# ScalarE's program of an attention stage, as a loop over pairs of steps and written out for all steps

## The chip, the cores and the metric

The kernel runs on one core of a Trainium2 chip. A core has five engines with a program each: TensorE (PE; its weight loads are shown apart as PEld), VectorE (DVE), ScalarE (ACT), GpSimd (POOL) and SyncE (SP). They meet only at semaphores. A small q behind an engine's name (ACTq) means its sequencer, which reads the program, sets registers, takes branches and issues DMAs. The metric is the device time of one execution in microseconds (us), the median of several; lower is better.

## The reference, cut to what matters

```
Q, K, V = Wq x, Wk x, Wv x                      # x: 8 batches, 512 channels, 1024 places; 16 heads of 32
att = softmax((Q K^T / sqrt(32) + b) masked by cond_2048)
y   = (att V) transposed                        # 8 x 512 x 1024
q   = per-row int8 quantisation of y            # absmax of a row / 127
out = x + f16(q W8^T * in_scale * w_scale + bias)
```

All matrix products of attention are computed in 32-bit floats; the quantised product runs in bf16.

## The kernel before, in words

The kernel has two stages, one after the other. `project` (to about 560 us) computes Q, K and V and stores them in DRAM. `attend` (line 504 on, from about 560 us to the end) does the rest in 32 steps: a step is one batch and one group of four heads. Line numbers here are those of the kernel before; behind line 867 those of the changed kernel are higher by one.

A step has 64 slots t. A slot is one pair of key tile (128 keys) and head, for one half of the queries (512). In slot t TensorE computes a block of scores (`scores`, L689) into one of three PSUM banks; ScalarE takes its exponential into `probs` in SBUF (`exps`, L798), which frees the bank; every fourth slot TensorE multiplies the four finished blocks of a key tile with V (`weigh`, L716, 8 matmuls into `pv`). Between them, in each slot, TensorE computes half of a pair of score blocks in the other orientation (`row_max`, L127), of which VectorE takes the row maxima (`reduce_max`, L136). These belong partly to this step and partly to the next.

In slots 23 and 55 the maxima are turned (L734), ScalarE and VectorE split them into two parts (`high_max` L803, `low_max` L877), and SyncE stores both parts with two small DMAs (L609) as rows of `q_stack`. TensorE waits for these rows in slots 32 and 0 (`max_rows`): the scores of that half need them. GpSimd sums the probabilities of a half (`add`, L987), after two accumulating DMAs of 1 MB that it issues itself (`begin_pair`, L971). In slot 51 TensorE does the quantised product for the step before (`ffn`, L749).

ScalarE also issues most loads (`loads`): K for the next step in slots 0 to 2 (L109), two bias rows (L115), V in slot 8 (L832), the second half of Q in slots 24 to 26 (L102), the residual in slot 30 (L843) and the first half of Q for the step after next in slots 38 to 40 (L102). It does these in its own order, between exponentials: while its sequencer issues a DMA, the next exponential isn't started.

Every engine runs its own order of work, written out by hand in a function `step(s, par, ...)`. `all_steps` (L585 to L594) calls it: steps -1, 0, 1 and 2 are written out, steps 3 to 28 are a loop of 13 rounds over two steps each (an odd one and an even one), and steps 29 to 32 are written out again. In the loop the step number is a register, so wait values and DMA addresses are computed by register instructions. TensorE, VectorE, ScalarE and GpSimd all use `all_steps`; SyncE has a loop of its own (L635).

Of the kernel before, what the change touches and what calls it, by code (L numbers as in the profile page):

```python
# [30 lines left out]
STEPS = B * G  # L31
# [472 lines left out]
def attend(nc, x, qk_d, v_d, bias_d, fw, ws_rep, fb_rep, out,  # L504
# [3 lines left out]
    with ExitStack() as ctx:  # L508
# [70 lines left out]
        def ring_of(par, use):  # L579

            return ring[(len(USES) * par + PLACE[use]) % 2]
# [3 lines left out]
        def all_steps(eng, body):  # L585

            body(-1, 1, main=False, prev=False)
            body(0, 0, prev=False)
            body(1, 1)
            body(2, 0)  # L590
            with eng.Fori(1, STEPS // 2 - 2) as pair:
                body(2 * pair + 1, 1)
                body(2 * pair + 2, 0)
            body(STEPS - 3, 1)  # L594
            body(STEPS - 2, 0)
            body(STEPS - 1, 1, ahead=False)
            body(STEPS, 0, main=False, ahead=False)
# [186 lines left out]
        def _(act):  # L784
# [15 lines left out]
            def high_max(s, chunk, buf):  # L800
                act.wait_ge(maxT_done, 2 * s + chunk + 1)
                wait(act, max_rows[chunk], MAX_ROWS * s)
                nc.scalar.activation(max_hi[:, chunk, :], buf[0:CHUNK, N:N + P], ACT.Copy).then_inc(max_hi_done, 1)  # L803

            def take_y(s, half):
                act.wait_ge(pv_done, QH * TT * s + (half + 1) * TT)
                wait(act, y_done, 2 * (s - 1) + half + 1)
                nc.scalar.activation(y_raw[:, half, :], pv[:, :], ACT.Copy).then_inc(y_raw_done, 1)

            def round_rows(s, half):  # L810

                cols = slice(half * N, (half + 1) * N)
                act.wait_ge(inv_done, s + 1)
                nc.scalar.activation(y[:, cols], y[:, cols], ACT.Identity, bias=magic[:, 0:1], scale=inv_scale[:, 0:1]).then_inc(rounded, 1)
# [26 lines left out]
            def load_res(s):  # L841
                wait(act, out_stored, 32 * s)
                act.dma_start(res[:, :], x[bass.ds(s * P, P), :]).then_inc(res_loaded, 16)  # L843

            def step(s, par, prev=True, main=True, ahead=True):
                for t in range(UNITS):
                    if main:
                        exps(s, t)
                        loads(s, par, t, prev, ahead)
                    elif t == 0 and prev:  # L850
                        load_res(s - 1)
                    if t == 3 and prev:
                        take_y(s - 1, 1)
                    if t == SUMS_1 and main:
                        high_max(s, 1, ring_of(par, ("extra", SUMS_1)))
                    if t == 35 and main:
                        take_y(s, 0)
                    if t in (37, 39) and prev:
                        round_rows(s - 1, (t - 37) // 2)
                    if t in (41, 43) and prev:  # L860
                        make_ints(s - 1, (t - 41) // 2)
                    if t == SUMS_0 and ahead:
                        high_max(s + 1, 0, ring_of(par, ("extra", SUMS_0)))

            act.wait_ge(const_set, 5)
            act.wait_ge(stack_set, 4)
            all_steps(act, step)

        @block.vector
        def _(dve):  # L870
# [225 lines left out]
```

## Time and profile before

| | |
|---|---|
| time, median of 3 runs (lowest to highest) | 2454.46 us (2453.87 to 2454.95) |
| the profiled execution, own time | 2455.09 us |
| its span (first to last instruction) | 2453.3 us |
| granted TensorE clock, mean | 0.99 |
| PE matmul busy | 2391.8 us, 97% |
| DVE busy | 1562.5 us, 64% |
| ACT busy | 1355.8 us, 55% |
| POOL busy | 1673.3 us, 68% |
| exponentials (L798) | 2048, 607 ns each |

Busy time of PE says that matmuls were in flight, not that PE was at its peak. What matters for a change in one engine's program is where TensorE waits for it, so the rows further down are taken from the chain of waits (the work that ended last, followed back from the end), from the timeline and from the list of one source line's instructions.

### The profile page before, as it was taken

How to read it: one execution, taken by the hardware profiler on the slowest of the kernel's cores; microseconds unless marked ns; L12 is line 12 of the kernel's file. 1: busy time of each engine (PE TensorE's matmuls, PEld its weight loads, DVE VectorE, ACT ScalarE, POOL GpSimd, SP SyncE). 2: the span in 40 equal slices, each digit the busy share in tenths (PEclk: the TensorE clock that was granted, in tenths of full speed). 3: DMA queues.
4: the chain of work that ended last, by engine and by line, in shares of the span. 5: the costliest groups of instructions: out<-in, count | busy, mean ns of one | idle time of the engine just before them, and what ended most of it. 6: DMA issues, size and time to landing. Idle time of an engine off the chain costs nothing.

```text
span 2453.3 us, 40026 instructions
## 1 busy us (share of the span) xinstructions
PE 2391.8 (97%) x12344; PEld 1342.7 (55%) x12376; DVE 1562.5 (64%) x1683; ACT 1355.8 (55%) x2536; POOL 1673.3 (68%) x677
## 2 busy tenths in 40 slices
PE   8999999997999999999999999999999999999997
PEld 7888888884444444444444444444444444444442
DVE  3311111155777777777777777777777777777771
ACT  3222222214666666666666666666666666666664
POOL 3322223414788888887788888887888888887786
PEclk9999999998999999999999999999999999999997
DMA  6655555465776667766777766667776667767751
GB/s 241 252 201 194 214 197 197 152 201 129 154 160 154 153 149 157 161 155 151 160 157 159 155 154 156 150 149 157 160 155 156 147 152 161 155 153 157 156 112 37
DMA packets 143540, 396.90 MB, mean 162 GB/s; under 512 B 14584, under 2 KB 50424, under 8 KB 127296
## 3 DMA queue, kind: packets, MB, share of 16 engines
q0 software_dynamic: 18144, 132.13, 26.9%
q10 hardware_dynamic: 49312, 130.80, 22.5%
q1 hardware_dynamic: 75968, 132.74, 14.8%
q8 instruction: 34, 0.56, 0.1%
q14 instruction: 82, 0.67, 0.1%
HBM read 161.51 MB, written 100.93 MB: 107 GB/s over the span
## 4 chain that ended last, share of the span: by engine, by line
PE 67%; issue 3%; DMA 3%; DVE 1%; ACT 1%; ACTq 1%; POOL 1%; SPq 0%; POOLq 0%; DVEq 0%
PE score L689 22%; PE pv L716 19%; PE ring L127 17%; PE ring L749 4%; DMA q_stack<-max_lo 3%; PE ring L726 2%; PE ring L729 2%; ACT probs L798 1%; DVE neg_max L136 1%; PE ring L740 1%; ACTq L102 1%; PE ring L734 0%; SPq L609 0%; DVE absmax L898 0%; POOL k_stack L121 0%
## 5 line engine op out<-in xcount | busy, mean ns | idle before, releaser
L798 ACT ACTIVATE probs<-score 128x512 f32<-128x512 f32 x2048 | 1085.7, 607 | 574.4 <-PE score L689 555.5
L136 DVE TENSOR_REDUCE neg_max<-ring 128x1 f32<-128x1024 f32 x1024 | 1210.4, 1221 | 242.2 <-PE ring L127 230.3
L689 PE MATMUL score<-q_stack,k_stack 100*128 100x512 f32 x2048 | 880.1, 432 | 30.3 <-DMA q_stack<-max_lo 15.8
L987 POOL TENSOR_TENSOR acc<-acc,probs 128x2048 f32<-128x2048 f32 x189 | 867.0, 4587 | 27.0 <-DMA probs<-probs 13.1
L127 PE MATMUL ring<-k_stack,q_stack 98*128 98x512 f32 x2048 | 811.0, 396 | 0.3 <-DVE neg_max L136 0.2
L689 PEld LDWEIGHTS score<-q_stack,k_stack 100*128 100x128 f32 x2048 | 388.8, 190 | 522.3 <-ACT probs L798 353.8
L716 PE MATMUL pv<-probs,v_in 128*32 128x512 f32 x4096 | 548.6, 608 | 0.0
L127 PEld LDWEIGHTS ring<-k_stack,q_stack 98*128 98x128 f32 x2048 | 390.7, 191 | 64.5 <-DVE neg_max L136 0.8
L987 POOL TENSOR_TENSOR acc<-probs 128x2048 f32<-128x2048 f32 x63 | 288.8, 4584 | 86.1 <-DMA probs<-probs 86.1
L479 POOL TENSOR_TENSOR q_stack<-x_raw,k_stack 128x1024 fp32r<-128x1024 f32 x28 | 67.7, 2456 | 293.1 <-ACT k_stack L364 293.1
L971 POOL DMA_DIRECT2D probs<-probs x126 | 108.6, 862 | 189.0 <-PE pv L716 182.3
L716 PEld LDWEIGHTS pv<-probs,v_in 128*32 128x32 f32 x4096 | 80.7, 108 | 185.9 <-issue 97.6
L435 DVE TENSOR_TENSOR part_lo<-score,part_hi 128x512 fp32r<-128x512 f32 x24 | 16.4, 691 | 179.5 <-ACT part_hi L389 179.5
L491 POOL TENSOR_TENSOR part_lo<-k_scaled,part_hi 128x512 fp32r<-128x512 f32 x64 | 83.3, 1320 | 55.0 <-ACT part_hi L392 55.0
L749 PE MATMUL ring<-fw,qT 128*128 128x512 bf16 x480 | 111.1, 385 | 6.2 <-issue 4.9
L1012 POOL TENSOR_TENSOR half<-prod,fb_rep 128x512 f16<-128x512 f32 x64 | 81.6, 1275 | 47.9 <-DVE prod L921 47.9
L291 PE MATMUL ring<-k_stack,w_hi 128*128 128x512 f32 x256 | 101.4, 396 | 0.0
L291 PE MATMUL ring<-k_stack,w_lo 128*128 128x512 f32 x256 | 101.2, 395 | 0.0
L291 PE MATMUL ring<-q_stack,w_hi 128*128 128x512 f32 x256 | 101.2, 395 | 0.0
L392 ACT ACTIVATE part_hi<-k_scaled 128x512 fp32r<-128x512 f32 x64 | 39.0, 628 | 111.3 <-DVE k_scaled L446 80.6
L921 DVE SCALAR_TENSOR_TENSOR prod<-ring,scale,ws_rep 128x512 f32<-128x512 f32 x64 | 48.1, 751 | 81.6 <-PE ring L749 81.6
L884 DVE STREAM_TRANSPOSE sums_turned<-ring 128x512 f32<-128x512 f32 x64 | 45.9, 717 | 83.7 <-PE ring L729 83.7
(95 smaller groups left out, 2031.1 us busy)
## 6 DMA issues: line engine op xcount, KB each, us to landing
probs<-probs POOLq DMA_DIRECT2D x126, 1024.0 KB, 7.8
k_stack<-qk_part ACTq DMA_DIRECT2D x93, 512.0 KB
q_stack<-qk_part ACTq DMA_DIRECT2D x183, 256.0 KB, 4.7
qk_part<-part_hi SPq DMA_DIRECT2D x64, 512.0 KB, 2.6
qk_part<-part_lo SPq DMA_DIRECT2D x64, 512.0 KB, 3.5
v_steps<-v_out SPq DMA_DIRECT2D x64, 256.0 KB, 2.2
res<-x ACTq DMA_DIRECT2D x32, 512.0 KB, 5.0
out<-res SPq DMA_DIRECT2D x64, 256.0 KB, 2.1
```

The lines of the kernel that those rows point to most:

```text
L127: mm = pe.matmul(ring[:, half * N:(half + 1) * N], q_stack[par][0:ROW_MAX, chunk, h, qt * P:(qt + 1) * P], k_stack[par][0:ROW_MAX, h, half ...
L136: nc.vector.tensor_reduce(neg_max[:, pair // CHUNK, pair % CHUNK:pair % CHUNK + 1], ring[:, :], AX_X, ALU.max, negate=True).then_inc(neg_m ...
L291: return pe.matmul(bank[:, :], lhsT, rhs, start=(k == 0), stop=(k == 3 * CT - 1))
L479: nc.gpsimd.tensor_tensor(x_lo[par][:, a, :], x_raw[:, a, :], x_hi[par][:, a, :].bitcast(F32), ALU.subtract).then_inc(x_lo_done, 1)
L491: nc.gpsimd.tensor_tensor(part_lo[:, g % 2, th * N:(th + 1) * N], k_scaled[:, i % 2, :], part_hi[:, g % 2, th * N:(th + 1) * N].bitcast(F3 ...
L689: pe.matmul(score[score_bank(t)][:, :], k_stack[par][0:ROWS, h, kt * P:(kt + 1) * P], q_stack[par][0:ROWS, half, h, :], start=True, stop=T ...
L716: mm = pe.matmul(pv[h * DH:(h + 1) * DH, :], v_in[:, par, kt % TT, h * DH:(h + 1) * DH], probs[:, kt % RING, h, :], start=(kt % TT == 0), ...
L749: mm = pe.matmul(buf[:, cols], qT[:, tt, :], fw[:, tt, cols], start=(tt == 0), stop=(tt == TT - 1))
L798: nc.scalar.activation(probs[:, kt, h, :], score[score_bank(t)][:, :], ACT.Exp).then_inc(exp_done, 1)
L971: pool.dma_start(probs[:, b, :, :], probs[:, a, :, :], accum_op=ALU.add).then_inc(pair_done[i], 16)
L987: nc.gpsimd.tensor_tensor(acc[:, half, :, :], first, probs[:, tile, :, :], ALU.add).then_inc(acc_done, 1)
L1012: nc.gpsimd.tensor_tensor(half16[:, half, :], prod[:, half, :], fb_rep[:, cols], ALU.add).then_inc(half_done, 1)
```

## The change

ScalarE doesn't call `all_steps` any more. It calls the same `step` once for each s from -1 to 32, with an ordinary number for s. The flags come out as `all_steps` has them. The other four engines keep their loops. The computation, the order of exponentials, copies and DMA issues and the conditions of all waits stay the same.

```
-            all_steps(act, step)
+            for s in range(-1, STEPS + 1):
+                step(s, s % 2, prev=s > 0, main=0 <= s < STEPS, ahead=s < STEPS - 1)
```

With numbers in place of a register the instructions that computed wait values and addresses are gone, and with the loop its branch. ScalarE's program of the stage gets longer: 1444 rows where the whole kernel's listing had 741.

The first place is ScalarE at the seam of two rounds of the loop, between an even step and the odd step behind it. Before, the last exponentials of the loop body and what closes it (the branch leads back to the row `L591 ISA` of the second listing):

```order
L798 ACTIVATE probs<-score 128x512
L797 REGISTER_ALU
L798 ACTIVATE probs<-score 128x512
L591 REGISTER_ALU
L591 COMPARE_AND_BRANCH
```

and the head of the loop body, where the odd step begins:

```order
L591 ISA
L73 ISA
L797 ISA
L798 ACTIVATE probs<-score 128x512
L109 ISA
L109 DMA k_stack<-qk_part 32x4x1024
L797 REGISTER_ALU
L798 ACTIVATE probs<-score 128x512
L109 DMA k_stack<-qk_part 32x4x1024
```

Now the same seam, from slot 55 of a step (L803) over its end into the next one:

```order
L803 ACTIVATE max_hi<-ring 16x128
L798 ACTIVATE probs<-score 128x512 x9
L109 DMA k_stack<-qk_part 32x4x1024
L798 ACTIVATE probs<-score 128x512
L109 DMA k_stack<-qk_part 32x4x1024
L798 ACTIVATE probs<-score 128x512
L109 DMA k_stack<-qk_part 32x4x1024
L798 ACTIVATE probs<-score 128x512
L808 ACTIVATE y_raw<-pv 128x512
```

The branch and the register rows are gone; the exponentials and the three K loads stand in the same order. (The L803 shown is that of slot 55; the nine exponentials behind it are slots 56 to 63 and slot 0 of the next step.)

The second place is ScalarE in slots 23 to 26, where it splits the maxima and issues three loads of Q. Before, in the loop:

```order
L803 ACTIVATE max_hi<-ring 16x128
L73 REGISTER_ALU x2
L797 REGISTER_ALU
L798 ACTIVATE probs<-score 128x512
L102 ISA
L102 DMA q_stack<-qk_part 32x4x512
L797 REGISTER_ALU
L798 ACTIVATE probs<-score 128x512
L102 DMA q_stack<-qk_part 32x4x512
L797 REGISTER_ALU
```

Now:

```order
L803 ACTIVATE max_hi<-ring 16x128
L798 ACTIVATE probs<-score 128x512
L102 DMA q_stack<-qk_part 32x4x512
L798 ACTIVATE probs<-score 128x512
L102 DMA q_stack<-qk_part 32x4x512
L798 ACTIVATE probs<-score 128x512
L102 DMA q_stack<-qk_part 32x4x512
L798 ACTIVATE probs<-score 128x512 x4
```

Here too only register instructions have gone; each Q load still stands between two exponentials. On TensorE, VectorE, GpSimd and SyncE nothing moved.

## Rows read from the trace of the kernel before

**Rows 1.** The page: part 1 (engine, busy us, share, instructions) and part 4.

```profile
PE 2391.8 (97%) x12344; PEld 1342.7 (55%) x12376; DVE 1562.5 (64%) x1683; ACT 1355.8 (55%) x2536; POOL 1673.3 (68%) x677
...
PE 67%; issue 3%; DMA 3%; DVE 1%; ACT 1%; ACTq 1%; POOL 1%; SPq 0%; POOLq 0%; DVEq 0%
```

**Rows 2.** Chain of waits, 974 to 979 us: start us, us, what.

```profile
974.23 2.41 issue
976.63 0.07 ACTq L591
...
976.91 0.61 ACT probs L798
...
977.56 0.50 PE score L689
```

**Rows 3.** Instructions of L591, 973 to 978 us: engine, operation, ns, first start.

```profile
L591 ACTq COMPARE_BRANCH  x1: 54/54/54, 974.2 to 974.2; - x1
...
L591 DVEq COMPARE_BRANCH  x1: 67/67/67, 974.4 to 974.4; - x1
L591 DVEq FUSED_REGOPS  x1: 85/85/85, 974.7 to 974.7; - x1
L591 ACTq FUSED_REGOPS  x1: 68/68/68, 976.6 to 976.6; - x1
```

**Rows 4.** Timeline of PE: start, us, engine, line, what, [idle before, releaser].

```profile
974.22 1.06 PE L716 MATMUL pv<-probs,v_in 128*32 128x512 f32 x8
...
977.56 0.50 PE L689 MATMUL score<-q_stack,k_stack 100*128 100x512 f32 x1 [0.68 <-ACT probs L798]
...
987.43 1.06 PE L716 MATMUL pv<-probs,v_in 128*32 128x512 f32 x8
...
1032.70 1.07 PE L716 MATMUL pv<-probs,v_in 128*32 128x512 f32 x8
...
1044.91 1.06 PE L716 MATMUL pv<-probs,v_in 128*32 128x512 f32 x8
```

**Rows 5.** Chain of waits, whole span: the quantised product, slot 51 of each step.

```profile
670.76 3.40 PE ring L749 x15
...
728.45 3.40 PE ring L749 x15
...
786.64 3.40 PE ring L749 x15
...
844.78 3.40 PE ring L749 x15
...
903.21 3.40 PE ring L749 x15
...
960.85 3.40 PE ring L749 x15
...
2237.77 3.40 PE ring L749 x15
...
2296.25 3.40 PE ring L749 x15
...
2354.02 3.40 PE ring L749 x15
```

**Rows 6.** Timeline, slots 26 to 32 of steps 4, 6, 29 and 30.

```profile
824.04 1.55 ACTq L102 DMA_DIRECT2D q_stack<-qk_part  x1
826.34 0.50 PE L689 MATMUL score<-q_stack,k_stack 100*128 100x512 f32 x1 [0.66 <-ACT probs L798]
...
940.59 0.78 ACTq L102 DMA_DIRECT2D q_stack<-qk_part  x1
...
944.58 0.49 PE L689 MATMUL score<-q_stack,k_stack 100*128 100x512 f32 x1 [0.24 <-DMA q_stack<-max_lo]
...
2280.03 0.50 PE L689 MATMUL score<-q_stack,k_stack 100*128 100x512 f32 x1 [1.21 <-DMA q_stack<-max_lo]
...
2333.51 1.45 ACTq L102 DMA_DIRECT2D q_stack<-qk_part  x1
```

## The prediction

> **What bounds the kernel now.** I read the page first. TensorE's matmuls are in flight for 97% of the span and PE is 67% of the chain that ended last; ScalarE is busy for 55% [rows 1]. So ScalarE isn't short of throughput, and a shorter program on it is worth only what TensorE loses by waiting for it. The chain's second entry, 3% of "issue", is time in which an engine waited for nothing that the profile shows. The reader should look for where it stands.
>
> In the chain it stands once in each round of the loop. At 974.23 us there are 2.41 us of issue, then ScalarE's sequencer works on L591 (the loop), the exponential of slot 0 starts at 976.91, and TensorE's score of slot 3, which waits for that exponential's bank, starts behind it at 977.56 [rows 2]. The list of the loop line's instructions shows whose time this is: ScalarE's branch is at 974.2 and its next instruction at 976.6, 2.4 us later, while VectorE takes its own branch at 974.4 and goes on at 974.7 [rows 3]. The hole belongs to ScalarE's branch alone and not to loops as such.
>
> The Trainium skill, "Runtime: NRT & Kernel Launch", section "Instruction fetch mechanics", says that a taken branch to a place outside the engine's small instruction window waits for a transfer of that page, and that kernels therefore prefer to be unrolled. The 2.4 us on the engine with the long body and 0.3 us on VectorE, whose body is shorter, fit it.
>
> **What the hole costs TensorE.** ScalarE's sequencer reaches the branch before its exponentials are through, so part of the 2.4 us is covered. TensorE's timeline gives the rest. A key tile is four slots. Across the seam four tiles take 974.22 to 987.43 = 13.21 us; across the middle of the loop body, between an odd and an even step, where ScalarE does the same work without a branch, four tiles take 1032.70 to 1044.91 = 12.21 us [rows 4]. The idle time before slot 3's matmul is 0.68 us, and the rest is pipelining that is lost. So one branch costs 1.00 us. The loop has 13 rounds, of which 12 end in a taken branch: 12.0 us at most.
>
> **What the change adds or moves.** No exponential, copy or DMA issue moves. The register instructions between exponentials go; most lay under exponentials. I cost them at nothing, and the bounds are in the step times below, since steps 2, 29 and 30 are written out already and hold none of them. What comes instead is a longer program to read, which I also take from those steps. Nothing new waits.
>
> **What is late next.** If ScalarE is in time at slot 0, TensorE runs 1 us ahead of where it was, and GpSimd's and SyncE's transfers don't all move with it. I therefore don't add up savings but take whole steps from the chain, where the quantised product stands once in each step at slot 51, so that a difference of two starts is one step [rows 5]:
>
> - Odd step behind a taken branch (step 5): 903.21 - 844.78 = 58.43 us.
> - Even step behind such a step (step 6): 960.85 - 903.21 = 57.64 us.
> - Steps in the loop with no taken branch in or just before them: step 3, 786.64 - 728.45 = 58.19; step 4, 844.78 - 786.64 = 58.14.
> - Steps written out: step 2, 728.45 - 670.76 = 57.69; step 29, 2296.25 - 2237.77 = 58.48; step 30, 2354.02 - 2296.25 = 57.77.
>
> The branch costs 1.00 us, but step 5 is only 0.29 longer than step 4, which has no branch before it. Something else is late in slots 26 to 32. The timeline shows two things there. In step 4 the third load of Q is 1.55 us in issue on ScalarE (824.04) and TensorE waits 0.66 us for the exponential behind it; in step 6 the same issue takes 0.78 us, and TensorE waits 0.24 us for the rows of maxima instead; in step 30, written out, the issue takes 1.45 us; in step 29 TensorE waits 1.21 us for the rows of maxima [rows 6]. So ScalarE's issue and SyncE's transfer stand side by side as the next limits, both fed by how busy the queues are. Part of what the branch costs is now time in which they catch up, and that part doesn't come back.
>
> **The sum.** The 26 steps 3 to 28 take 2237.77 - 728.45 = 1509.32 us [rows 5]. Changed, all 26 are written-out steps without a branch. The nearest rows are steps 2 and 30, 57.69 and 57.77, mean 57.73: 26 x 57.73 = 1501.0, which is 8.3 us less. Step 29 is the third written-out step and 0.75 us over that mean. I let two of the 26 be like it, plus 1.5 us; it is one of three before, but the only one whose maxima were that late. That leaves 6.8, say 7 us. The stages outside stay. The profiled execution took 2455.09 us; less 7 is 2448.1. The median of the runs is 0.63 below the profiled one, so the changed kernel's median should be 2447.5 us, 0.28% less.
>
> Bounds: all 26 steps like step 6 and a little better (the whole 12.0 us returned) gives 2442.5. All like steps 3 and 4 (mean 58.17) gives 26 x 58.17 = 1512.4, 3.1 us more: 2457.5. All like step 29 gives 26 x 58.48 = 1520.5, 11.2 us more: 2465.6. The value taken is nearest to the written-out steps 2 and 30, because they are the same code as all steps will be and stand in the same surroundings.
>
> **Rivals.**
>
> 1. All of it returns: 12 x 1.00 us, median 2442.5. For it: steps like 6 show that slots 26 to 32 can be nearly free. Against it: step 6 stands behind a step that was delayed, and steps 3, 4 and 30, which don't, have the long third issue.
> 2. The middle of the step takes it all back: every step is like 3 and 4, median 2457.5, or between those and the forecast. For it: these two are the only pair in a row without any branch stall in the steady part, and what they show may be how queues settle when nothing relieves them. Against it: they still have register instructions around the issues, and steps 2 and 30 are 0.4 us shorter. Half-way between (57.95 a step) it is 2453, no change to speak of.
> 3. Slower, by one mechanism: the rows of maxima land late in most steps, as in step 29, because ScalarE's now continuous reading of new program adds transfers beside GpSimd's accumulating DMAs. Price 0.75 us a step over the forecast, up to 2465.6; it decides against the change once the mean step is over 58.24 us (1509.32 + 4.9 over 26), which is two steps in three like step 29. Against it: steps 2 and 30 read new program too and don't show it.
> 4. The stall at the seam isn't the branch's but that of a new step's first work, and stays: 2454.5. Against it: the seam in the middle of the body has the same work and no hole [rows 4].
>
> On rival 3, the Trainium skill, "DMA: Bandwidth & Descriptors", section "Queues, rings and completion order", says that each DMA engine goes round the queues that have work, a packet at a time. By that rule every page of program read in slots 16 to 32 would make one engine's share of the accumulating DMA late, and a transfer is as late as its latest share. No row here shows such a read beside a late landing. How often it would fall there decides between the forecast and this rival.
>
> **Chances.** Forecast (5 to 10 us less) 0.52; rival 1 (over 10 less) 0.15; rival 2 (4.9 less to 4.9 more) 0.22; rival 3 (over 4.9 more) 0.07; rival 4 0.04. This kernel's measurement can tell about 0.2%, 4.9 us, from no change. So faster: 0.52 + 0.15 = 0.67, less 0.03 for the forecast's own edge near 5 us: 0.64. Same: 0.22 + 0.04 + 0.03 = 0.29. Slower: 0.07. The range goes from 2442.0, just under the full return, to 2455.0, which takes in most of rival 2.
>
> **What would show each step.** The branch: in the chain the 2.4 us issue once in 116 us is gone, and four key tiles across any step's start take 12.2 us; ScalarE's list has no L591 compare-and-branch in this stage. If a hole of over 1 us shows elsewhere on ScalarE, program reading isn't hidden. The middle of the step: distances between the quantised products should be near 57.7, odd and even alike, in place of 58.43 and 57.64 in turn. If they are near 58.15, rival 2 holds, and the third Q issue will be about 1.5 us with TensorE behind it; near 58.5 with waits of over 1 us for the rows of maxima, rival 3. The forecast is wrong in its reasoning, even with a right time, if TensorE doesn't gain at the seam, or if slots 26 to 32 don't wait longer than they do now in even steps.

## The result, and the profile after

| | before | after |
|---|---|---|
| time, median of 5 runs (lowest to highest) | 2453.87 us (2452.07 to 2454.95) | 2440.84 us (2438.5 to 2442.08) |
| the profiled execution, own time | 2455.09 us | 2440.84 us |
| its span | 2453.3 us | 2439.0 us |
| granted TensorE clock, mean | 0.99 | 0.993 |

The changed kernel takes 0.9947 of the time before [0.9936, 0.9958]: 13.0 us or 0.53% less. I had forecast 2447.5 us with a range from 2442.0 to 2455.0. The direction was right, the size wrong by a factor of two, and the time lies outside the range, 1.2 us below its lower end. Ratios and medians in this document leave out one run, of `q_late_loop`, which took 2618.68 us at a mean granted clock of 0.847.

The page of the changed kernel, with the lines that answer to [rows 1] and the queue on which ScalarE's program is read (queue, kind: packets, MB, share):

```profile
PE 2387.2 (98%) x12376; PEld 1341.0 (55%) x12376; DVE 1560.4 (64%) x1683; ACT 1346.3 (55%) x2536; POOL 1672.1 (69%) x677
...
q14 instruction: 40, 0.33, 0.0%
...
PE 67%; DMA 4%; issue 2%; POOL 2%; DVE 2%; ACT 0%; SPq 0%; ACTq 0%; POOLq 0%; DVEq 0%
```

and the same queue on the page of the kernel before:

```profile
q14 instruction: 82, 0.67, 0.1%
```

"Issue" has fallen from 3% to 2% of the chain, ACT and ACTq from 1% each to nothing. The written-out program isn't more reading: 40 packets here, where the loop took 82, since the loop read its body anew in each round.

The chain of waits of the changed kernel, whole span, at the quantised product of each step (start, us, what). The first, third, fourth and last rows answer to those of [rows 5]:

```profile
729.50 3.56 PE ring L749 x16
787.12 3.56 PE ring L749 x16
845.11 3.56 PE ring L749 x16
902.43 3.56 PE ring L749 x16
960.01 3.56 PE ring L749 x16
1017.84 3.56 PE ring L749 x16
...
2225.41 3.56 PE ring L749 x16
2284.19 3.56 PE ring L749 x16
2341.89 3.56 PE ring L749 x16
```

Steps 3 to 28 take 2225.41 - 729.50 = 1495.91 us, where they took 1509.32 [rows 5]: 13.4 us less, as much as the medians differ. The mean step is 57.54 us. By differences of all starts, odd steps fell from 58.41 to 57.47, even ones from 57.70 to 57.60: what the branch had cost has gone from the steps behind it, and next to nothing has come back.

The timeline of the changed kernel (start, us, engine, line, what, [idle before, releaser]): two of TensorE's products with V around the start of step 7, which is the seam of [rows 4], then the third load of Q and the wait behind it in step 7, and the same load in step 19:

```profile
973.58 1.07 PE L716 MATMUL pv<-probs,v_in 128*32 128x512 f32 x8
...
985.79 1.06 PE L716 MATMUL pv<-probs,v_in 128*32 128x512 f32 x8
...
997.42 1.51 ACTq L102 DMA_DIRECT2D q_stack<-qk_part  x1
...
999.63 0.50 PE L689 MATMUL score<-q_stack,k_stack 100*128 100x512 f32 x1 [0.41 <-ACT probs L798]
...
1688.26 0.78 ACTq L102 DMA_DIRECT2D q_stack<-qk_part  x1
```

Four key tiles across the seam take 985.79 - 973.58 = 12.21 us, exactly what they take in the middle of the old loop body, where they took 13.21 at the seam [rows 4]. The long third issue of [rows 6] is there in step 7 with its 0.41 us of waiting, and not in step 19.

I summed TensorE's records over steps 3 to 28 by the slots in which the time lies. Slots 28 to 35 mean the eight intervals from the start of slot 27's score block to that of slot 35's:

| steps 3 to 28, us | before | after | difference |
|---|---|---|---|
| slots 28 to 35, sum of 26 steps | 168.37 | 169.19 | +0.8 |
| of it per odd step | 6.32 | 6.43 | +0.11 |
| of it per even step | 6.63 | 6.59 | -0.05 |
| slots 39 to 43 | 95.1 | 93.5 | -1.6 |
| everywhere else | | | -12.6 |
| in all | 1509.32 | 1495.91 | -13.4 |

"Everywhere else" is the seam: 12.5 of the 12.6 us are lost in front of slots 3 and 4. Take the time from slot 59's score block to that of slot 7 of the next step, once for each of the 26 steps. Before, it is 10.10 to 10.40 us in front of the 12 odd steps that stand behind a taken branch, and 9.15 to 9.19 in front of the other 14. Among the 14 are all 13 even steps, which run such register instructions at that place too, with no branch among them. After, all 26 take 9.16 to 9.31. So the loss at the seam goes with the branch, and the register instructions show no part in it.

One more difference lies in the two profiles alone. A row by stretches of each kernel (window, us, then busy us of PE, PEld, DVE, ACT and POOL, granted clock, DMA share, GB/s), in step 31. Before, with the seam of step 7 ahead of it for use further down:

```profile
974.20:976.60 2.40, 2.40 (x15) 1.22 (x14) 1.70 (x3) 0.57 (x2) 2.40 (x1) 1.00 0.01 3
...
2395.20:2407.60 12.40, 12.40 (x36) 3.95 (x36) 0.25 (x2) 9.32 (x17) 12.11 (x3) 0.50 0.00 1
```

After, a stretch that includes the same work:

```profile
2379.70:2397.00 17.30, 13.67 (x71) 4.86 (x70) 1.76 (x4) 14.18 (x28) 16.29 (x5) 1.00 0.14 41
```

The execution of before that was profiled had TensorE at half its clock for 13.7 us there, which cost it 3.7 us by the intervals of its key tiles; the one of after hadn't. The first experiment below shows the same drop in a kernel with the gain, so it belongs to an execution and not to the change. Steps 3 to 28 lie before it, and their 13.4 us don't contain it.

### The profile page after: what moved, and what is told of

Its sections match the earlier page's. It is cut to its first block, busy times and chain, and to the rows that moved or that the text cites. A ratio compares the mean times of both kernels' runs of the same rounds, so it can differ in the third digit from the quotient of the medians.

```text
span 2439.0 us, 37390 instructions
## 1 busy us (share of the span) xinstructions
PE 2387.2 (98%) x12376; PEld 1341.0 (55%) x12376; DVE 1560.4 (64%) x1683; ACT 1346.3 (55%) x2536; POOL 1672.1 (69%) x677
## 4 chain that ended last, share of the span: by engine, by line
PE 67%; DMA 4%; issue 2%; POOL 2%; DVE 2%; ACT 0%; SPq 0%; ACTq 0%; POOLq 0%; DVEq 0%
PE score L689 21%; PE pv L716 18%; PE ring L127 18%; PE ring L749 4%; DMA q_stack<-max_lo 4%; PE ring L726 2%; PE ring L729 2%; DVE neg_max L136 1%; PE ring L740 1%; POOL acc L988 1%; PE ring L734 0%; DMA probs<-probs 0%; POOL acc L1000 0%; ACT probs L798 0%; SPq L609 0%
## 5 line engine op out<-in xcount | busy, mean ns | idle before, releaser
L798 ACT ACTIVATE probs<-score 128x512 f32<-128x512 f32 x2048 | 1074.7, 604 | 576.4 <-PE score L689 559.5
L689 PE MATMUL score<-q_stack,k_stack 100*128 100x512 f32 x2048 | 875.8, 429 | 23.9 <-DMA q_stack<-max_lo 16.6
L749 PE MATMUL ring<-fw,qT 128*128 128x512 bf16 x512 | 117.8, 384 | 0.9 <-DVE qT L917 0.9
```

Of the source, the lines that this page charges most:

```text
L689: pe.matmul(score[score_bank(t)][:, :], k_stack[par][0:ROWS, h, kt * P:(kt + 1) * P], q_stack[par][0:ROWS, half, h, :], start=True, stop=T ...
L749: mm = pe.matmul(buf[:, cols], qT[:, tt, :], fw[:, tt, cols], start=(tt == 0), stop=(tt == TT - 1))
L798: nc.scalar.activation(probs[:, kt, h, :], score[score_bank(t)][:, :], ACT.Exp).then_inc(exp_done, 1)
```

## Experiments

Each was run beside the kernel before on the same chip. The medians of before there were 2454.25 us (beside `one_round`, `four_steps`, `seam_52` and `q_late`), 2452.94 us (beside `seam_20`, `q_late_loop`, `pe_out` and `dve_four`), 2454.09 us (beside `sp_loop`, `sp_out` and `dve_six`) and 2454.16 us (beside `q_late_pe`). The label stands in the title of each.

**One round of a loop (`one_round`).** Is it the branch, or the register instructions in the loop, that cost time? This kernel was meant to keep registers for all waits and addresses of steps 3 to 28, without a taken branch.

```
-            all_steps(act, step)
+            with act.Fori(1, 2) as once:
+                for j in range(STEPS - 6):
+                    step((STEPS - 6) * once - (STEPS - 9) + j, (j + 1) % 2)
```

(Steps -1 to 2 and 29 to 32 are written out around it, here and in the next ones.)

> ScalarE's steps 3 to 28 stand in a loop of one round, 26 steps long: the step number is a register and all register instructions of the old loop are there, but no branch is ever taken. Theory A (the taken branch is the loss, 12 times 1.00 us, and register instructions cost next to nothing): within 2 us of the written-out kernel, so 11.5 to 13.5 us below the kernel before, about 2441.5. Rival B (a good part of the gain comes from the register instructions between exponentials and DMA issues, since the gain was 13.0 us and not 7): steps 3 to 28 stay 0.15 to 0.4 us longer each, 4 to 10 us above the written-out kernel, 2445 to 2451. In the trace both expect no 2.4 us of issue; A expects 57.5 to 57.6 us a step, B 57.7 to 58.1.

Measured: 2442.86 us (2440.71 to 2443.39), ratio 0.9948 [0.9934, 0.9961]. Its chain of waits at the quantised products of steps 2 and 28:

```profile
729.73 3.56 PE ring L749 x16
...
2225.81 3.56 PE ring L749 x16
```

1496.08 us, against 1495.91 written out. But the experiment doesn't do what it was built for. These are the sequencer's instructions of the line that computes the wait values of the exponentials (L797, from 728 to 2240 us), first in the kernel before, then in `one_round`, and then all that `one_round` has of its loop's line:

```profile
L797 ACTq ALU_OP  x1627: 35/35/44, 743.9 to 2236.6; - x181
...
L797 ACTq EVENT_SEMAPHORE  x419: 38/38/38, 733.6 to 2237.9; - x140
...
L869 ACTq MOVE  x1: 42/42/42, 743.2 to 743.2; - x1
...
L869 ACTq COMPARE_BRANCH  x1: 48/48/48, 2239.3 to 2239.3; - x1
```

The changed kernel has the same 419 waits there, and none of either has register arithmetic. A loop of one round was turned into the written-out program, with one branch at its end that isn't taken. So `one_round` is a second sample of the change, and a close one (0.2 us in 26 steps), and says nothing about register instructions. What parts the two is the comparison of seams above, and `sp_loop` and `sp_out` further down, where branches and register instructions stay and the hole doesn't: there the two together are worth 1.3 us. Put on the branches alone, the difference to the kernel before is (1509.32 - 1496.08) / 12 = 1.10 us each. The granted clock was 0.51 in this profile too in step 31 (2383 to 2397 us).

**Four steps to a round (`four_steps`).** Five taken branches in place of twelve.

```
+            with act.Fori(1, 7) as four:
+                for j in range(4):
+                    step(4 * four - 1 + j, (j + 1) % 2)
```

> ScalarE's loop has four steps in a round and six rounds, so five taken branches in place of twelve; it is otherwise the old loop, steps 27 to 32 are written out. Theory A (each taken branch costs 1.0 to 1.1 us, whatever stands behind it): 5 x 1.05 = 5.3 us above the written-out kernel, 2446, or 7.5 below the kernel before. Rival C (a delayed step leaves the queues emptier and gives part back in slots 26 to 32 of this and the next step, as the prediction had it): the steps without a branch are then longer, 57.9 or more, and the time is 2448 or more. The branch is expected once in 231 us with a hole of about 2.4 us.

Measured: 2448.32 us, ratio 0.9973 [0.9963, 0.9984]. The hole stands in its chain of waits once in four steps:

```profile
975.75 2.41 issue
```

Steps 3 to 28 take 1502.92 us, 6.8 more than with one round, which is 1.4 us for each of the five branches: 1.05 at the seam, the rest mostly in slots 39 to 47. So the loss at the seam follows the number of branches: this loop keeps the register instructions of 24 steps, and only the five seams with a taken branch cost. The median is 2.3 us above what theory A had and stands in the range of rival C, but not by C's mechanism: from step 5 to step 27, steps without a branch in front took 57.3 to 57.8 us, and C needed 57.9 and more.

**The seam in slot 52 (`seam_52`).** The same loop of two steps, turned, so that the branch stands behind slot 51 of the odd step, where SyncE's and GpSimd's transfers are under way.

```
-            def step(s, par, prev=True, main=True, ahead=True):
-                for t in range(UNITS):
+            def step(s, par, prev=True, main=True, ahead=True, first=0, last=UNITS):
+                for t in range(first, last):
...
+            step(3, 1, last=SEAM)
+            with act.Fori(1, STEPS // 2 - 2) as pair:
+                step(2 * pair + 1, 1, first=SEAM)
+                step(2 * pair + 2, 0)
+                step(2 * pair + 3, 1, last=SEAM)
+            step(STEPS - 3, 1, first=SEAM)
```

> ScalarE's loop of two steps a round with twelve taken branches as before, but turned so that the branch stands behind slot 51 of the odd step, where TensorE does the quantised product and ScalarE waits over 3 us for scores anyway. Theory A (the branch costs because nothing covers its 2.4 us at slot 0): the hole is still in ScalarE's program but no longer on the chain, and the kernel is within 2 us of the written-out one, 2440 to 2443. Rival D (reading the loop's head again adds transfers, 42 more instruction reads than the written-out kernel by the page's queue rows, and these cost by themselves): 3 to 6 us above the written-out one, 2444 to 2447. If it is like the kernel before, 2454, the branch isn't the cause.

Measured: 2453.1 us (2452.22 to 2456.66), ratio 0.9996 [0.9987, 1.0005]: the time of before. I had written that such a time would clear the branch. It doesn't, since the branch's hole didn't stay as it was. The chain of waits has a longer one than [rows 2]:

```profile
1015.89 6.40 issue
```

and its stretch shows why it costs TensorE no more than it does, and what else was going on:

```profile
1015.90:1020.80 4.90, 4.90 (x27) 2.19 (x27) 2.52 (x4) 0.52 (x2) 1.91 (x2) 1.00 1.04 214
```

TensorE had other work for these 4.90 us. The DMA share is 1.04, where it was 0.01 in the hole of before (the first stretch of before, above). In the records of the DMA queues the read of the next piece of program starts 4.92 us after the branch here and 0.93 us in before. Steps 3 to 28 take 1509.68 us. Slots 28 to 35 fall to 164.02 us in all (even steps 6.23 us each, in place of 6.59), and everything else takes 18.8 us more than with one round, 1.6 a branch, nearly all of it in front of slots 55 and 56. So the giving back that I had forecast is real, but for a branch in this place, and it's the even steps that have it: 5.2 of 18.8 us. What is left is 13.6 us, 1.1 a branch, as in the kernel before.

**The seam in slot 20 (`seam_20`).** The same edit with another number, so that the branch stands ahead of the Q loads, with the accumulating DMAs under way and no quantised product for TensorE to be busy with.

```
+            SEAM = 20
```

> ScalarE's loop turned so that its branch stands behind slot 19 of the odd step: no pause of ScalarE there beyond the usual 1 us a key tile, and GpSimd's accumulating DMA in flight (DMA share 0.9 to 1.0 at that place of the step, against 0.01 at the old seam). Theory F (the 2.4 us at slot 0 and the 6.4 us at slot 52 are the same read of program, which waits behind data in the DMA queues): the hole is 4 to 7 us here, TensorE loses it less 1.4 us, 12 times, which is 30 to 65 us more than the written-out kernel: 2471 to 2506. Rival G (the 6.4 us of slot 52 had to do with something at that slot, and the read takes 2.4 us elsewhere): 1.0 us a branch, 2452 to 2455.

Measured: 2521.67 us, ratio 1.0282 [1.0268, 1.0297], 2.8% slower, and above what either theory had. The chain of waits:

```profile
994.67 6.14 issue
```

the stretches under the hole and behind it:

```profile
994.70:999.00 4.30, 2.62 (x15) 1.18 (x14) 3.44 (x5) 0.51 (x2) 0.86 (x1) 1.00 1.01 208
...
1001.00:1004.50 3.50, 2.74 (x10) 0.70 (x10) 1.22 (x1) 2.08 (x4) 3.50 (x1) 0.61 0.91 190
```

and the timeline there:

```profile
1001.76 0.80 PE L689 MATMUL score<-q_stack,k_stack 100*128 100x512 f32 x1 [4.44 <-ACT probs L798]
...
1002.92 1.94 PE L716 MATMUL pv<-probs,v_in 128*32 128x512 f32 x8
```

The hole is 6.2 us, nearly as long as in slot 52, with the DMA share at 1.01 (the read starts 4.66 us after the branch). So its length goes with the traffic in the three places tried; that part of the expectation held. The price didn't. By the chain's products in slot 51 steps 3 to 28 take 1577.17 us (2304.70 - 727.53), 6.8 us a branch. That is more than the hole: TensorE is idle for 4.44 us, and then its clock is granted at half for 3.4 to 6.8 us each time. The score block behind the gap takes 0.80 us and the eight products with V 1.94 us, where they took 0.50 and 1.06 [rows 4].

**Q loads late (`q_late`).** The table of slots says that 6.13 us, the shortest that any step shows for slots 28 to 35, is missed by 0.4 us a step. This is the changed kernel with the three loads of slots 24 to 26 in slots 32 to 34.

```
-                if ahead and t in (24, 25, 26):
-                    load_q(act, qk_d, q_stack, s + 1, 1 - par, 1, t - 24, q2_loaded)
+                if ahead and t in (32, 33, 34):
+                    load_q(act, qk_d, q_stack, s + 1, 1 - par, 1, t - 32, q2_loaded)
```

> The written-out kernel, with ScalarE's three loads of the second half of Q moved from slots 24, 25, 26 to slots 32, 33, 34. It takes away both things that are late in slots 26 to 32: the long third issue, and traffic beside the rows of maxima. If these are the next limit (the prediction's second step), slots 28 to 35 take 6.13 to 6.3 us in place of 6.5 on the mean, and 29 steps give 6 to 11 us: 2430 to 2435. Rival E (the accumulating DMA of GpSimd alone decides when the rows of maxima land, and the third issue is a mere witness): even steps keep 6.5 us there and the kernel gains under 3 us, 2438 to 2441. It can be slower, 2443 or more, if the Q loads now push the first half of Q or the accumulating DMAs of the second half.

Measured: 2424.28 us (2423.79 to 2427.12), ratio 0.9878 [0.9863, 0.9893], 30 us below before and 6 us below the least that was expected. The chain of waits:

```profile
724.51 3.56 PE ring L749 x16
...
2210.62 3.56 PE ring L749 x16
```

Steps 3 to 28 take 1486.1 us, 9.8 less than with the change alone. Slots 28 to 35 are 6.13 to 6.19 us in every step from 3 to 28, and step 29 is 57.20 us, where it was 58.78. Another 7 us came outside these steps: 1.0 before step 0, 4.0 in steps 0 to 2 (step 0 alone 53.8 in place of 57.7), 2.0 from step 29 on. So what was late in slots 26 to 32 hangs on these three loads. Whether it is ScalarE's stop for the issues or the traffic of the loads beside the rows of maxima isn't shown, since the edit takes away both. By place it is about half each: of the 9.7 us that slots 28 to 35 lose, 5.1 are in front of slots 30 and 31, which wait for exponentials, and 4.7 in front of slot 32, which waits for the rows.

**Q loads late, with the loop (`q_late_loop`).** The kernel before with only this edit: is the branch still worth its 1.1 us when nothing can take it back?

> The kernel before, loop and all, with the three Q loads moved from slots 24 to 26 to slots 32 to 34. With slots 26 to 32 waiting for nothing, nothing can be given back there. Theory A (a branch costs TensorE 1.0 to 1.1 us, and the middle of the step neither gave back nor took much): 12 x 1.05 = 12.6 us above the written-out kernel with late Q loads (2424.3), 2436 to 2438. Rival C (the middle of the step gave part of the branch back): the difference is clearly larger than the 13.0 us between the two kernels of this case, 15 us or more, 2439 or more. Slots 28 to 35 are expected at 6.13 to 6.2 us in all steps.

Measured: 2438.61 us (2435.63 to 2439.61), ratio 0.9938 [0.9925, 0.9951]. The chain of waits:

```profile
725.63 3.56 PE ring L749 x16
...
2225.69 3.56 PE ring L749 x16
```

1500.06 us, 14.0 more than without the loop: 1.16 us for each of 12 branches, against 1.10 in the kernel before. The medians differ by 14.3. The time lies between what the two theories expected, close to that of a branch that costs 1.1 us whatever the middle does. Slots 28 to 35 were 168.37 us before and are 159.47 here, so the three loads cost 8.9 us in 26 steps with the loop and 9.7 without it: nearly the same. The two edits add up: 0.53% and 0.62% alone, 1.22% together.

**TensorE's program written out too (`pe_out`).** In both kernels step 29 is long (58.48 us [rows 5] and 58.78) and has a 16 KB read of TensorE's program 20 us behind its start. If such reads hurt, more of them hurt more.

```
-            all_steps(pe, step)
+            for s in range(-1, STEPS + 1):
+                step(s, s % 2, prev=s > 0, main=0 <= s < STEPS, ahead=s < STEPS - 1)
```

> The written-out kernel with TensorE's program written out for all steps too. TensorE's loop had no hole at its branch, so nothing is gained there; its program is then read anew through the whole stage, in reads of 16 KB about every 17 to 20 us. Theory H (a read of program that falls into the 17 to 26 us behind a step's start makes the accumulating DMA and the rows of maxima late, as in step 29, whose slots 28 to 35 took 7.5 us before and 7.8 after): about every second step has such a read, slots 28 to 35 take 7 us or more there, and the kernel is 5 to 20 us slower than the written-out one, 2446 to 2460. Rival I (reads of program cost nothing, and step 29 is long for another reason): 2439 to 2443, and slots 28 to 35 stay at 6.5 us on the mean.

Measured: 2437.43 us (2436.15 to 2439.89), ratio 0.9942 [0.9929, 0.9955]; 3.1 us below the 2440.51 us of `dve_four` on the same chip, which (further down) has the time of the changed kernel. That is below the ranges of both theories. The theory that more reads of TensorE's program cost more time is false: there are 93 packets on that queue in place of 34, two or three in each step, 0.5, 12.6, 26, 36 or 52 us behind its start, and steps 3 to 28 take 1494.5 us. The chain of waits shows where it gained:

```profile
2222.67 3.56 PE ring L749 x16
...
2280.08 3.56 PE ring L749 x16
```

Step 29 is 57.41 us, 1.4 less: its reads now fall at 12.6 and 36 us. Step 31 lost 1.0 us too, in slots 28 to 35, where its read at 21 us is gone.

**VectorE's loop with four steps to a round (`dve_four`).** VectorE's loop has 189 instructions a round and its hole is 0.3 us [rows 3], ScalarE's has 419 and 2.4 to 2.7. Size, or engine? This is the changed kernel with `four_steps`'s loop on VectorE, 373 instructions.

> The written-out kernel, with VectorE's loop at four steps a round in place of two (about 190 instructions a round before, 380 now; ScalarE's old loop had 419 and a hole, VectorE's had none). Theory J (a branch is free as long as the loop's head is still held by the sequencer, and the hole comes with a body that is too long, on any engine): VectorE's instruction behind its branch comes 2.3 to 2.7 us later in place of 0.12 us, five times, and TensorE waits for a row of maxima there, 0.5 to 1.5 us each: 2.5 to 7 us slower than the written-out kernel. Rival K (the hole is peculiar to ScalarE): 0.12 us at VectorE's branch and no difference in time.

Measured: 2440.51 us, ratio 0.9949 [0.9935, 0.9964], the time of the changed kernel. The instructions of the loop's line, on VectorE's sequencer (engine, operation, ns, first start):

```profile
L956 DVEq COMPARE_BRANCH  x1: 74/74/74, 974.6 to 974.6; - x1
L956 DVEq FUSED_REGOPS  x1: 85/85/85, 974.9 to 974.9; - x1
```

0.3 us, as before. So 373 instructions are still at hand when the branch goes back.

**VectorE's loop with six steps to a round (`dve_six`)**, 557 instructions. It ran once, so its time, 2442.0 us, isn't compared.

```
+            with dve.Fori(1, 5) as six:
+                for j in range(6):
+                    step(6 * six - 3 + j, (j + 1) % 2)
```

> The written-out kernel with VectorE's loop at six steps a round: about 560 instructions a round; with four steps it was 374 and there was no hole. Theory J' (the hole comes when a round is longer than what a sequencer holds, and that lies between VectorE's 374 and ScalarE's 419): a hole of 1 to 3 us, or over 5 if data transfers are under way, at each of VectorE's three taken branches (about 1090, 1435 and 1780 us). Rival K (peculiar to ScalarE): 0.12 us there as before.

```profile
L956 DVEq COMPARE_BRANCH  x1: 74/74/74, 1089.1 to 1089.1; - x1
L956 DVEq FUSED_REGOPS  x1: 85/85/85, 1091.9 to 1091.9; - x1
```

2.8 us from branch to next instruction, on another engine (2.8 to 3.1 at its three branches). The hole goes with the body's length and isn't peculiar to ScalarE.

The same trace shows something more. VectorE's longer program is read at places of its own, and in steps 10, 16 and 22 one such 8 KB read starts 20.2 to 20.3 us behind the step's start. The third load of Q in step 8, which has no such read, and in step 10:

```profile
1055.32 0.96 ACTq L102 DMA_DIRECT2D q_stack<-qk_part  x1
...
1170.29 1.57 ACTq L102 DMA_DIRECT2D q_stack<-qk_part  x1
```

In the three steps that issue takes 1.57 to 1.65 us and slots 28 to 35 take 6.89 to 6.96; in the other even steps from 6 to 26 it takes 0.89 to 0.99 and they take 6.34 to 6.44. The same three steps of the changed kernel have no such read, and take 6.59, 6.58 and 6.49.

**All loads issued by SyncE, with the loop (`sp_loop`).** ScalarE's loads (K, bias, V, Q, residual) move to SyncE's program, the second half of Q late; all loops stay, SyncE's with its last steps written out. ScalarE's body has 355 instructions, register instructions included. The main parts of the edit:

```
-                        loads(s, par, t, prev, ahead)
...
+                if main and ahead:
+                    wait(sp, score_done, UNITS * s)
+                    for k in range(3):
+                        load_k(sp, qk_d, k_stack, s + 1, 1 - par, k, k_loaded)
...
+                    sp.wait_ge(score_done, UNITS * s + UNITS // 2 + 1)
+                    for k in range(3):
+                        load_q(sp, qk_d, q_stack, s + 1, 1 - par, 1, k, q2_loaded)
```

> The kernel before, loops and all, with all of ScalarE's loads (K, bias rows, V, Q, residual) issued by SyncE instead, the Q loads of the second half behind slot 32. ScalarE's loop body is then about 355 instructions in place of 419, branch and register instructions kept. Theory J' (length decides): no hole at ScalarE's twelve branches (under 0.3 us), slots 28 to 35 at 6.13 us, 2420 to 2428. Rival K: the hole stays 2.4 us, and the kernel is 11 to 13 us above the next one, 2433 to 2440.

Measured: 2427.43 us (2423.4 to 2427.67), ratio 0.9887 [0.9871, 0.9904]. The instructions of the loop's line:

```profile
L591 ACTq COMPARE_BRANCH  x1: 45/45/45, 969.4 to 969.4; - x1
...
L591 ACTq FUSED_REGOPS  x1: 68/68/68, 969.6 to 969.6; - x1
```

0.24 to 0.26 us in all twelve rounds, and no read of ScalarE's program in the steady rounds. Steps 3 to 28 take 1487.45 us. By itself this kernel would leave open whether the shorter body or the missing DMA issues closed the hole; VectorE's two sizes answer that.

**The same, ScalarE written out (`sp_out`).**

> As the one with SyncE's loads, with ScalarE's program written out. Theory J': equal to the looped one within 2 us, since there is nothing left to gain from writing out, 2420 to 2428. Rival K: 11 to 13 us faster than the looped one. Against the written-out kernel with late Q loads on ScalarE (2424.3) both expect 0 to 4 us less, since ScalarE no longer stops for issues.

Measured: 2425.37 us (2424.15 to 2425.64), ratio 0.9883 [0.9867, 0.99]; steps 3 to 28 take 1486.10 us. The change of this document, made on a kernel whose loop body is short enough, is worth 1.3 us by the traces, 0.1 a branch, and nothing that the intervals tell apart. That 1.3 us is all that twelve held branches and the register instructions of 26 steps cost together in this kernel. Against `q_late` I had expected 0 to 4 us less; it is 1.1 more, which the intervals don't tell apart from nothing.

**Both edits, TensorE written out (`q_late_pe`).**

> The written-out kernel with the Q loads in slots 32 to 34 and TensorE's program written out too. TensorE's writing out alone was worth 3.4 us on the median, of which 1.4 us is step 29 and 1.4 us the slots 28 to 35 of steps 3 to 28. Theory L (it acts only where a read of program meets the accumulating DMA and the rows of maxima, and late Q loads have taken the waiting there away): nothing left, 2423 to 2426 like the kernel with late Q loads alone (2424.3). Rival M (something else is saved): 2 to 4 us less, 2420 to 2422.

Measured: 2424.19 us (2422.6 to 2426.26), ratio 0.9875 [0.9858, 0.9891], the time of late Q loads alone. What `pe_out` gained up to step 30, it gained in slots 26 to 32, and there is nothing left there (steps 3 to 28 take 1486.47 us). Step 31 still gains: its slots 28 to 35 take 5.5 us in place of 6.6. The versions with late Q loads, `q_late`, `q_late_pe` and `sp_out`, are the fastest and aren't told apart.

## Why the prediction was off, step by step

**What bounds the kernel: right.** The page, the chain's "issue" once a round and the branch's instructions named the place. 12.5 of the 13.4 us went from the twelve seams behind a taken branch, and the seams in the middle of a round, with such register instructions and no branch, had nothing to lose. `four_steps` has the loss five times, and `sp_loop` keeps branches and register instructions and loses the hole. Rival 4 (the stall is that of a new step) is out.

**What the hole costs TensorE: right, a little low.** I had 1.00 us and 12.0 in all; at the seam it is 12.5, 1.04 a branch, and 1.10 with what it takes with it elsewhere. Four tiles across the seam take the 12.2 us that I had put down as the sign.

**What the change adds: right.** The register instructions cost nothing at the seams, and with twelve branches at most 1.3 us in all in `sp_loop`. My own bound for them, the written-out steps 2, 29 and 30, was none, as the sum below shows. The longer program added no hole anywhere on ScalarE.

**What is late next: this is the term that was wrong.** I had about 5 us of the 12 come back in slots 26 to 32, and 0.8 us did. The two things I saw there, the long third Q issue and the late maxima, exist; `q_late` shows that the three loads cost every step 0.4 us. But they cost 0.3 us before the change already. My own sign says so: the reasoning is wrong if slots 26 to 32 don't wait longer than they did in even steps. They took 6.63 us there, and now take 6.43 in odd and 6.59 in even steps. To take back time at a second place, the second place has to be passed by slack that the first one makes. What I had was one comparison, step 5 against step 4, and step 4 isn't an undisturbed step: it is as long in the changed kernel (6.99 us in slots 28 to 35, against 7.08), where later steps take 6.5.

**The sum: rows that stand for nothing.** I sized the term by whole steps at the edges: 2, 3, 4, 29 and 30, as the steps without a branch. They are all longer than what the steady part shows without one, 57.54 us: 26 x 57.73 and the 1.5 us for two steps like 29 make 1502.5 us, 6.6 more than the 1495.91 that came. That is the step that failed, and about the whole error of the forecast. Slots 28 to 35, where an undelayed step of the changed kernel mostly takes 6.2 to 6.6 us:

| step | before, us | after, us | read of program 19 to 22 us behind the step's start |
|---|---|---|---|
| 2 | 6.67 | 6.76 | none |
| 3 | 7.07 | 6.54 | before: 8 KB at 21.6 |
| 4 | 7.08 | 6.99 | both: 8 KB at 20.3 |
| 7 | 6.40 | 6.83 | 8 KB, before at 20.4, after at 19.5 |
| 13 | 6.23 | 6.84 | 8 KB, before at 20.3, after at 19.6 |
| 19 | 6.14 | 6.23 | 8 KB, before at 20.3; after at 14.0 |
| 29 | 7.46 | 7.76 | both: 16 KB (TensorE), before at 20.5, after at 19.8 |
| 30 | 6.74 | 6.68 | none |

In before steps 3 and 4 are the first round of the loop, in which ScalarE's program reads its body for the first time, at other moments than in later rounds. Step 29 is the first step behind TensorE's loop. So three of my five rows had a read at a moment at which the even steps inside the loop have none, and the steady odd steps, which take 6.13 to 6.40, show that they weren't typical either. Better rows were there: the steps of the loop themselves, mended. 13 even ones of 57.70 us, and 13 odd ones of 58.41 less twelve branches of 1.00, make 750.1 + 759.3 - 12.0 = 1497.4 us, within 1.5 us of what came.

**The late reads (rival 3): not a bound, but not nothing.** `pe_out` moved TensorE's read in step 29 and the step lost 1.4 us; in the changed kernel the three steps in the loop's place whose 8 KB read falls at 19.5 to 20.3 us (4, 7 and 13) have slots 28 to 35 of 6.83 to 6.99, the other 23 a mean of 6.46. The third Q issue is 1.5 us in step 7 and 0.8 in step 19, whose read is at 14 us. With late Q loads the same reads at 19.6 us (steps 7 and 13) cost nothing: 6.13. `dve_six` has the same in three steps that had no such read before: 0.5 us each, with the third Q issue at 1.6 (a correlation too: each of them is also the second step behind a hole of VectorE's). Two things speak against a simple form. Before, all odd steps had a read at 20.3 us, behind a seam that was 1 us late, and took 6.13 to 6.40; and `one_round` takes 6.81 in step 7 and 6.61 in step 13 with the same reads. So rival 3 names something that seems to be there, at 0.4 to 0.5 us a step, but in few steps of the changed kernel: 3 of 26. On the rule of the Trainium skill that each DMA engine goes round its queues by the packet ("DMA: Bandwidth & Descriptors", section "Queues, rings and completion order"): a share of a transfer made late by such a read would look like this, and no run here shows the share itself.

**The chances.** The full return had 0.15 and a price of 2442.5, and it is the case that came, 1.7 us better. Of this, 0.6 us is that the median of before is 2453.87 with more runs, and 1.0 that the gain was 13.0 and not 12.0: the range ended just under the price, with no room for a seam that costs 12.5 us or for slots 39 to 43, which gave another 1.6 us (0.06 a step). That last part doesn't belong to the branch: steps 3 and 4, which have no branch in front, take 3.67 and 3.65 us there before and 3.60 and 3.59 after, while in `four_steps` only the first two of a round's four steps have it. What it is, is open.

Open, too: why steps 2 and 30 are longer, with no read in the window (it lies in slots 28 to 35: with late Q loads they take 57.2 and 57.1 us like the rest); and how a read does what it does.

## What to carry to other kernels

A loop costs by its length and its place. With a body that the sequencer still has at hand (373 instructions here) the branch is 0.2 to 0.3 us, and writing the loop out is worth next to nothing; past that (419 here) each round waits 2.4 us and more for its own beginning, so shorten the body, make the rounds long, or choose the seam: where the DMA queues are idle the hole is short, and where other engines have work it is covered. (The two places tried with one of these each cost the same 1.1 us; none with both was run.) Don't size a term by the steps next to a loop, which read their program at other moments than those inside: take the loop's own steps and mend them. And before something "late next" is charged to a change, ask whether it isn't paid already: here it was, and three DMA issues moved by eight slots were worth more (16.6 us) than the loop. Last, look into the trace of a control before reading its time: the loop of one round, built to keep register instructions, had none.

## What the runs showed that I had not expected

**A missed branch is as long as the queues are full.** Time from ScalarE's branch to its next instruction:

| kernel | instructions a round | branch in | DMA share there | read starts after | hole | cost a branch, all told |
|---|---|---|---|---|---|---|
| sp_loop | 355 | slot 0 | | no read | 0.24 us | 0.1 us |
| before | 419 | slot 0 | 0.01 | 0.93 us | 2.4 to 2.7 us | 1.1 us |
| seam_52 | 420 | slot 52 | 1.04 | 4.92 us | 6.4 us | 1.1 us (1.6, less 0.4 given back) |
| seam_20 | 418 | slot 20 | 1.01 | 4.66 us | 6.2 us | 6.8 us |

On the rule of the Trainium skill, "Runtime: NRT & Kernel Launch", section "Instruction fetch mechanics", that a taken branch out of a small window waits for a transfer: the traces agree, with a body of 373 instructions inside on VectorE and 557 outside, 355 inside on ScalarE and 419 outside. The page has a window of 512 instructions for these engines, and the 419 are fewer. Whether the rest of the window was taken by what had been read ahead isn't shown; for a loop the measurement decides, and the limit lies between 373 and 419 instructions of the trace.

**A short idle of TensorE can cost more than itself.** 4.44 us of idleness in slot 20 was followed each time by 3.4 to 6.8 us at the lower granted clock (1.2 in place of 2.4 GHz): 0.61 mean over a stretch that includes the change of level. The 2.4 us holes at the seam, in which TensorE idles for 0.68 us (step 7), left it at 1.00.

**Some executions have TensorE at 0.5 in step 31.** In the profiles of before and `one_round` it is 13.7 us long, in `q_late_loop` 6.8, in `q_late` 3.4, and in the one of the changed kernel there is none. The same program can do either, it seems: of the five runs of the changed kernel four have a mean granted clock of 0.992 or 0.993, and the slowest, 2442.08 us, has 0.990, like the profile of before. A drop of 13.7 us cost 3.7 us of time. A difference of two profiles has to be read by stage because of it.
